# Two attention layers: heads split into high and low parts on 96 rows, against plain float32 heads on a quarter of the rows each

## What is computed

```python
scores = jnp.einsum('bqhd,bkhd->bhqk', q, k) * scale          # second layer, H = 16 heads of 8
scores = jnp.where(causal[None, None], scores, -inf)
attn = jax.nn.softmax(scores, axis=-1)
ctx = jnp.einsum('bhqk,bkhd->bqhd', attn, v)

ctx = X @ We.T                                                # third layer
influence = jnp.einsum('bqe,bke->bqk', ctx, ctx)
scores = jnp.einsum('bhqd,bhkd->bhqk', Q, K) * SCALE + 0.1 * influence[:, None]
attn = jax.nn.softmax(scores, axis=-1)
```

## Time and profile before

| | |
|---|---|
| median of 3 runs | 1821.09 us (1820.46 to 1821.55) |
| the profiled execution | 1818.61 us |
| its span, first to last instruction | 1816.9 us |
| busy: PE, DVE, ACT, POOL | 84%, 69%, 57%, 44% of the span |
| mean granted TensorE clock | 0.907 of full speed |

### The profile page before, as it was taken

How to read it: one execution, slowest core, us unless ns; L and a number is a source line. 1 busy time by engine, 2 the same in 40 slices (tenths; PEclk the granted TensorE clock), 3 DMA queues, 4 the chain that set the end, 5 groups by cost and what they waited for, 6 DMA issues and landing times. The chain is left out here.

```text
span 1816.9 us, 26731 instructions
## 1 busy us (share of the span) xinstructions
PE 1527.4 (84%) x8757; PEld 964.7 (53%) x8757; DVE 1249.6 (69%) x3212; ACT 1027.1 (57%) x1749; POOL 793.7 (44%) x902
## 2 busy tenths in 40 slices
PE   3788888689999999588769999999997686999980
PEld 1444555466666666343335545555553565777770
DVE  1656667467777777267777778777882574888875
ACT  2444555335666655424636677677675554777762
POOL 2244534435555544324741111222001576688875
PEclk8888989759999999788868999999998698999995
DMA  6800000212222221000244444443530022344415
GB/s 214 278 1 1 1 1 1 61 60 78 69 74 72 70 73 35 4 14 1 72 107 122 109 110 121 120 120 92 131 72 1 32 68 90 117 126 136 126 55 139
DMA packets 96201, 144.30 MB, mean 79 GB/s; under 512 B 31266, under 2 KB 59939, under 8 KB 91952
## 3 DMA queue, kind: packets, MB, share of 16 engines
q1 hardware_dynamic: 91072, 134.11, 26.5%
q0 software_dynamic: 4992, 8.48, 1.4%
HBM read 104.19 MB, written 57.48 MB: 89 GB/s over the span
## 5 line engine op out<-in xcount | busy, mean ns | idle before, releaser
L1176 DVE TENSOR_REDUCE ctx_nm<-ctx_s 128x1 f32<-128x512 f32 x496 | 320.0, 681 | 87.4 <-PE ctx_s L1310 86.6
L1176 DVE TENSOR_REDUCE rope_nm<-rope_s 128x1 f32<-128x128 f32 x496 | 223.5, 481 | 83.0 <-PE rope_s L1313 80.7
L1554 ACT ACTIVATE rope_probs<-rope_st 128x1024 f32<-128x1024 f32 (+1 forms) x256 | 172.2, 702 | 139.1 <-PE rope_st L1657 137.9
L1554 ACT ACTIVATE ctx_probs<-ctx_st 128x1024 f32<-128x1024 f32 x192 | 190.3, 1023 | 87.6 <-PE ctx_st L1657 84.1
L1310 PE MATMUL ctx_s<-att_kst,att_qst 96*128 96x512 f32 x496 | 210.9, 459 | 19.4 <-DVE ctx_nm L1176 8.4
L1310 PE MATMUL rope_s<-att_kst,att_qst 96*128 96x128 f32 x496 | 179.0, 392 | 8.8 <-PEq L120 5.5
L1657 PE MATMUL ctx_st<-att_qst,att_kst 98*128 98x512 f32 x512 | 164.7, 404 | 2.4 <-ACT ctx_probs L1554 1.5
L1419 POOL TENSOR_SCALAR_AFFINE_SELECT rope_probs<-rope_probs 128x256 f32<-128x256 f32 x256 | 98.1, 408 | 156.1 <-ACT rope_probs L1554 155.6
L1310 PEld LDWEIGHTS ctx_s<-att_kst,att_qst 96*128 96x128 f32 x496 | 95.8, 193 | 127.3 <-DVE ctx_nm L1176 51.0
L1657 PE MATMUL rope_st<-att_qst,att_kst 98*128 98x512 f32 (+3 forms) x512 | 141.2, 360 | 3.9 <-ACT rope_probs L1554 3.9
L2930 DVE TENSOR_TENSOR sw_hl<-sw_hf,sw_hh 128x512 fp32r<-128x512 f32 x124 | 128.5, 1037 | 0.1
(11 more groups left out here) (429 smaller groups left out, 3467.1 us busy)
## 6 DMA issues: line engine op xcount, KB each, us to landing
sw_raw<-in_L_ffn_all SPq DMA_DIRECT2D x24, 768.0 KB, 4.4
sw_xs<-in_pad SPq DMA_DIRECT2D x65, 260.0 KB, 9.5
rope_halves<-att_qk SPq DMA_DIRECT2D x24, 512.0 KB
ctx_halves<-att_qk SPq DMA_DIRECT2D x24, 512.0 KB, 5.7
att_qst<-ctx_contexts SPq DMA_DIRECT2D x32, 384.0 KB
att_kst<-ctx_contexts SPq DMA_DIRECT2D x32, 384.0 KB
att_qst<-rope_halves SPq DMA_DIRECT2D x32, 192.0 KB
att_kst<-rope_halves SPq DMA_DIRECT2D x32, 192.0 KB
```

The source lines that it names most:

```text
L1176: nc.vector.tensor_reduce(nm[:, g, j * T + t:j * T + t + 1], bank("s", b, n)[:, 0:keys], AXX, ALU.max, negate=True).then_inc(s_used, 1)
L1554: nc.scalar.activation(prob(n // GH % 2, n % GH)[:, u * units[0]:u * units[0] + units[u]], st_bank[u][:, 0:units[u]], ACT.Exp, scale=SCALE ...
```

## The change

The stacks become float32 tiles of 128 rows, `kst` and `qst` of shape [128, 2, NG, S], two batches deep. Head j of every group lies in quarter j of the rows: 8 rows of the head, in the third layer 16 of the context, and the guard in the last row of the quarter (row 31 of 32). `halves_of`, `halves_of_context`, `clear_stacks`, `guard_of_ones`, `cut_guard` and the float32r tiles go; `store_parts` and `load_stacks` write and read one batch whole, and `turn_guard` turns the maxima in one instruction. `prepare` sets the stacks and `vaug` at the start of the Performer's block on POOL.

A step now has four products, two heads by key and two by query, on four different quarters: those by key first, with keys c = i // 2 and heads of half i % 2, then those for the maximum, of the other half, with the query block whose width is the same; in the causal layer the two bfloat16 products (`hide_future` of PE) follow behind both. All other small products of the causal layer move from the bank `side` into the ring of three `s` banks; `st` becomes two tiles of two banks. The exponential takes two heads of one key block at a time. The Performer's `yT`, `yb`, `qT`, `kT`, `qp`, `qpT` and `hT` get tiles of their own.

```diff
-        self.kst, self.qst = sb("kst", [STACK + 2, NG, GH, S], F32R), sb("qst", [STACK + 2, NG, GH, S], F32R)
+        self.kst, self.qst = sb("kst", [P, 2, NG, S]), sb("qst", [P, 2, NG, S])
...
+        def scored(n):
+            i, k = n // 2, n % 2
+            return 2 * (1 - i % 2) + k, T - 1 - i // 2 if causal else i // 2
...
-                        (side if SIDE else ring).append((name, own, 0))
+                        ring.append((name, own, 0))
...
+            def load_stacks(b):
+                if causal and b == 0:
+                    sp.wait_ge(init, 4)
+                sp.wait_ge(stored, (b + 1) * NS)
+                for side, st in enumerate((qst, kst)):
+                    src = parts[b, side].rearrange("(d g j) t -> j d g t", g=NG, j=GH)
+                    for j in range(GH):
+                        row = QUARTER * j
+                        sp.dma_start(st[row:row + DH, b % 2], src[j]).then_inc(stacks_loaded[b % 2], 16)
+                        if not causal:
+                            sp.dma_start(st[row + DH:row + DH + CE, b % 2], contexts[b, side].unsqueeze(1).broadcast_to([CE, NG, S])).then_inc(stacks_loaded[b % 2], 16)
...
+            def prepare():
+                for k in range(2):
+                    nc.gpsimd.memset(qst[:, k], 0.0).then_inc(init, 1)
+                    nc.gpsimd.memset(kst[:, k], 1.0).then_inc(init, 1)
...
+            def turn_guard(b, g):
+                n = b * NG + g
+                dve.wait_ge(s_used, b * 64 + (g + 1) * GH * T)
+                if n:
+                    dve.wait_ge(m_stored, n * 16)
+                nc.vector.transpose(cutT[:], nm[:, g]).then_inc(mT_ready, 1)
...
+            def scores(b, pair):
...
+                two = (2 * pair, 2 * pair + 1)
+                g = pair // PAIRS
+                for n in two:
+                    vacated("s", b, n)
+                    j, t = scored(n % (GH * T))
+                    keys = P * (t + 1) if causal else S
+                    rows = slice(QUARTER * j, QUARTER * j + GUARD)
+                    last = nc.tensor.matmul(bank("s", b, n)[:, 0:keys], qst[rows, b % 2, g, t * P:(t + 1) * P], kst[rows, b % 2, g, 0:keys],
+                                            start=True, stop=not causal)
+                    if not causal:
+                        last.then_inc(s_ready, 1)
+
+            def hide_future(b, pair):
+                for n in (2 * pair, 2 * pair + 1):
+                    keys = P * (scored(n % (GH * T))[1] + 1)
+                    nc.tensor.matmul(bank("s", b, n)[:, keys - P:keys], identb[:], maskb[:], start=False, stop=True).then_inc(s_ready, 1)
...
+            def scores_by_key(b, g, i):
+                m = (b * NG + g) * PAIRS + i
+                if i == 0:
+                    pe.wait_ge(m_loaded[g % 2], (b * NG // 2 + g // 2 + 1) * 16)
+                if m >= 2:
+                    pe.wait_ge(p_ready, m - 1)
+                c, half = i // 2, i % 2
+                for k in range(2):
+                    rows = slice(QUARTER * (2 * half + k), QUARTER * (2 * half + k + 1))
+                    last = nc.tensor.matmul(st_bank[half][:, k, 0:width[c]], kst[rows, b % 2, g, c * P:(c + 1) * P],
+                                            qst[rows, b % 2, g, S - width[c]:S], start=True, stop=True)
                 last.then_inc(st_ready, 1)
...
-                    if within(ahead[0]) and not lead(ahead):
-                        score(*ahead, j, 2 * u)
                     now = keys_step(b, h)
                     if now:
-                        scores_by_key(now[0], now[1] // 8, j, u)
+                        scores_by_key(*now)
                     if within(ahead[0]) and not lead(ahead):
-                        score(*ahead, j, 2 * u + 1)
-                    if within(behind[0]) and u == 1 and j in (1, 3):
-                        weigh_values(*behind, j - 1)
-                        weigh_values(*behind, j)
+                        scores(ahead[0], ahead[1] * PAIRS + i)
+                    if within(ahead[0]) and not lead(ahead) and causal:
+                        hide_future(ahead[0], ahead[1] * PAIRS + i)
+                    if within(behind[0]) and i in (3, 7):
+                        weigh_values(*behind, i // 4 * 2)
+                        weigh_values(*behind, i // 4 * 2 + 1)
```

380 lines of the change are left out of this document (132 added, 248 removed).

## The result

| | before | after |
|---|---|---|
| median | 1820.78 us (4 runs, 1815.92 to 1821.55) | 2039.27 us (4 runs, 2035.32 to 2043.18) |
| ratio, 95% interval | | 1.1206, 1.1175 to 1.1238 |
| profiled execution: span | 1816.9 us | 2039.6 us |
| from first to last score of the causal layer | 373.2 to 728.0: 354.8 us | 378.5 to 857.0: 478.5 us |
| the same, third layer | 933.8 to 1366.5: 432.7 us | 1064.2 to 1585.5: 521.3 us |

The kernel is 12% slower. The prediction had 2012 us, slower, with a range of 1890 to 2160. Direction and range held, and so did the mechanism in the causal layer; in the third layer two of its steps did not, and the size fell 27 us short. Of the 222.7 us between the two spans, 123.7 lie in the causal layer (forecast 118), 88.6 in the third (69) and 10.4 in the seams and the rest (4).

The account below looks back on a forecast made before the run. PE was taken to set the causal layer's pace, DVE and PE the third's. Waits add 118 us causal, 69 third, 4 seams: 191 on the profiled 1818.6, the median 2.5 above, 2012 us, range 1890 to 2160.

Parts of the forecast that it names:

- the seams: Outside the two main blocks: +6 at the Performer's end, about 0 at the mixture's end, -2 for stack clearing; +4 us.
- The bound and the arithmetic: PE paces the causal layer, DVE and PE the third; four products cost 0.85 us of columns before and after.
- The causal chain: Causal layer: second product, bfloat16 product, first reduction, next second product wait in turn; 12.4 us a group.
- its smaller terms: Causal layer, per group: value products 2.4, hidden waits -1.5, transposes and projections in the ring +1.1, DVE's other work 0.65.
- the +6 for the start: Causal layer's first 28.8 us, at clock 0.52: two groups come to 37 us where 30 were counted.
- Rival 3: Clock stays at 1.2 GHz through both layers: +330 and +345, 2500 us; chance 0.09 in long stretches.
- The third layer: Longer stops at value products and small products, less the cuts, slower first steps: +69 us together.
- value products: Third layer: DVE stands 2.2 us at each of 62 places, 1.4 before; +50 us.
- transposes, projections: Third layer: eight a batch need four quarters drained and refilled, half a microsecond each; +31 us.
- the cuts: Third layer: the cuts go, 9.1 + 5.5 us of an engine that is the bound; -15 us.
- between value products DVE can run without a stop at 0.65 us a reduction: Third layer: the first bank can be read before the second is full, so no loss there.
- The signs: PE waits for `rope_nm` in over 200 places, DVE idles near 165 us in the third layer, starts within 0.05 us.

Follow-up runs that it names:

- a_short: The changed kernel with every reduction of both layers reading only the first 128 columns of its bank: 1903.06 us, ratio 1.0460 to the kernel before.
- a_nomask: The changed kernel without the bfloat16 products that hide later keys from the maximum: 1939.31 us, ratio 1.0652 to the kernel before.
- a_values4: The changed kernel with value products of one key block behind each second step, not two behind each fourth: 2006.13 us, ratio 1.1022.
- b_ring: The kernel before with the causal layer's small products in the ring of three banks instead of a bank of their own: 1846.36 us, ratio 1.0043.
- b_nomask: The kernel before without the bfloat16 products of the causal layer: 1822.48 us, ratio 0.9914.
- a_sf_halves: The changed kernel with scores for the maximum ahead of those by key, and the heads of the two halves exchanged: 2295.76 us, ratio 1.2488.
- a_scoresfirst: The changed kernel with products for the maximum and bfloat16 products ahead of the products by key: 2294.71 us, ratio 1.2592.

## Why the prediction was right, and where it was short

**The bound and the arithmetic** held. Four products on four row quarters start within 0.02 us and take 0.86 us of columns at 512, as the value products do on column quarters; a step of them alone takes 1.07 us, 0.11 of load and 0.11 of emptying around the columns:

```profile
1300.28 0.70 PE L1600 MATMUL ctx_st<-att_qst,att_kst 32*128 32x512 f32 x2
1300.29 0.70 PE L1280 MATMUL ctx_s<-att_kst,att_qst 31*128 31x512 f32 x2
...
1300.81 0.59 PE L1600 MATMUL ctx_st<-att_qst,att_kst 32*128 32x512 f32 x2
...
1301.35 0.66 PE L1238 MATMUL ctx_s<-ident,ctx_y 128*128 128x128 f32 x4
```

The page TensorE: Matmul & The Clock Gate of the Trainium skill, "Part 3: Packing small matmuls", gives 3.07 times; the trace has four times for the columns and 3.2 with load and emptying (4 x 0.86 over 1.07). The prediction counted both apart, so its value was right.

**The causal chain**, 12.4 us of a group, is shown: turns within 0.02 us behind a pair of the same width, its reduction taken away by a_short, its bfloat16 product by a_nomask, the cover that value products have by a_values4. A batch's four groups take 13.8, 14.2, 16.8 and 15.4 us wherever the clock is full, 15.05 on the mean, as forecast. That its smaller terms, which no run measured one by one in the changed kernel, are each right is not shown (the +6 for the start is 37 less 30, so 7; it measured 35.4 for the 37); b_ring had 0.3 us a group for one of them where 1.1 was counted, in a kernel with single products instead of pairs.

**The clock** took the causal layer past its forecast. Rival 3 had it low in long stretches or nowhere. In fact it fell seven times in the main part, for 3 to 7 us each, and came back. (The prediction also read from the earlier trace rows that before the change it "rose as the value products began"; in the trace it rose at 400.7 us, 1.2 us ahead of them, and after the change at 418.1, 4.7 us ahead.) The changed kernel, in stretches of 2.5 us, and what PE did as it fell:

```profile
642.50:645.00 2.50, 2.50 (x29) 1.38 (x26) 1.03 (x3) 1.54 (x4) 0.69 (x2) 1.00 0.00 0
645.00:647.50 2.50, 2.47 (x28) 1.49 (x26) 1.52 (x7) 1.76 (x6) 1.36 (x3) 0.85 0.00 0
647.50:650.00 2.50, 2.50 (x24) 0.74 (x16) 0.15 (x1) 0.00 (x0) 2.47 (x6) 0.50 0.07 13
650.00:652.50 2.50, 2.50 (x16) 0.82 (x12) 1.93 (x6) 1.83 (x2) 0.41 (x1) 0.96 0.02 3
```

```profile
644.46 0.28 PE L1288 MATMUL rope_s<-rope_maskb,rope_identb 128*128 128x128 bf16 x2
644.68 0.38 PE L1600 MATMUL rope_st<-att_qst,att_kst 32*128 32x128 f32 x2
...
645.62 0.28 PE L1288 MATMUL rope_s<-rope_maskb,rope_identb 128*128 128x128 bf16 x2
645.84 0.38 PE L1600 MATMUL rope_st<-att_qst,att_kst 32*128 32x128 f32 x2
```

Each of the seven falls comes within 0.6 us of the last bfloat16 product of the two steps of 128 columns that end a group; but all 29 groups end so, and 22 of them kept the clock. The value products that follow a fall run at 1.2 GHz. In all 27 of the 434.2 us passed at half clock. Beside groups at the same place in other batches, the groups with a fall are longer by 12 us together. Without the falls the layer would be at 467 us where 355 and 118 are 473, so the other terms together were 6 us too high.

**The third layer** is the part that failed: +88.6 for +69. DVE's idle time before its reductions, sorted by the PE products that started between the start of the last reduction and this one's:

| PE between | before | after | more | forecast |
|---|---|---|---|---|
| value products | 70.8 us | 115.2 us | 44 | 50 |
| transposes, projections | 10.2 us | 30.7 us | 20 | 31 |
| steps alone | 0.4 us | 18.2 us | 18 | 0 |
| the cuts, DVE's own time | | | 0 | -15 |

(The idle times are of the main part of the layer; +7 us more lie ahead of it, for +3. The line between the second row and the third is a matter of counting: from the end of the last reduction on, steps alone have 10.7 us before and 42.0 after.) Two steps of the forecast failed.

The first is "between value products DVE can run without a stop at 0.65 us a reduction". Here is a stretch without other work, and four reductions in a row of the kernel before:

```profile
1484.85 2.59 DVE L1153 TENSOR_REDUCE ctx_nm<-ctx_s 128x1 f32<-128x512 f32 x4 [2.05 <-PE ctx_s L1280]
1485.59 0.29 PEld L1280 LDWEIGHTS ctx_s<-att_kst,att_qst 31*128 31x128 f32 x2 [0.79 <-DVE ctx_nm L1153]
...
1487.65 1.29 DVE L1153 TENSOR_REDUCE ctx_nm<-ctx_s 128x1 f32<-128x512 f32 x2 [0.21 <-PE ctx_s L1280]
```

```profile
1333.26 2.48 DVE L1176 TENSOR_REDUCE ctx_nm<-ctx_s 128x1 f32<-128x512 f32 x4
```

The first reduction frees its bank at 1485.54, and the reduction of that bank's next use starts at 1486.75, 1.21 us later. The forecast's own terms give 0.06 + 0.11 + 0.86 + 0.22 = 1.25 for this, and DVE has two reductions to do meanwhile. Back to back their starts are 0.60 us apart, not 0.65, so these two take 1.21 us as well. Nothing is left over, and the next bank, freed at 1486.14, has its next reduction only 1.52 us later: DVE stops for 0.02 and then for 0.21 us. The main part has 55 stops like the first and 28 like the second. Why the second refill takes longer no run shows. a_short, whose reductions take 0.28 us, brought 64 us in this layer; it does not part these stops from those at the value products.

The second is the -15 for the cuts. They went, and all of DVE's instructions in this layer last 382.9 us after and 395.7 before. But back to back they overlap by 0.08 us, in 611 places before and in 461 after, so that the time in which DVE runs at all is the same, 346.4 and 346.0 us. The 60 cuts overlapped their neighbours and so cost about 10 us, not 15 (14.6 less 60 times 0.08). And DVE starts from rest 91 times more often than before, each time without the 0.08: about 7 us. Those took what the cuts gave.

**The seams** had 10.4 us for 4: 5.3 up to the causal layer's first score in the main block (forecast 4), 1.4 at the mixture's end (0), 3.7 behind the third layer, which the prediction did not count.

**The signs** it named: DVE idle before each pair, PE's wait for `rope_nm` (136 places in the list of waits, not over 200), DVE's idle time near 165 (175.9), starts within 0.05 us. All but the one count came.

## What to carry to other kernels

Equal columns are not equal time. Before putting products side by side, walk the ring: from a bank's release to the moment it is full again, and count what the reader has left to read meanwhile; here both were 1.21 us in the third layer, and DVE stopped even in quiet stretches. Products side by side lengthen that way, since all columns come late together (1.21 us from a product's start to its reduction, where one float32r product took 0.54), and here each product over all rows had 0.1 us of emptying on either side. And look at what PE's granted clock does in the thinnest stretch of the loop, not at its mean.

## What was not expected of the hardware

The granted clock changed with the order and the rows of the same instructions: 0.97 in the causal main part with keys first, 0.66 with scores first, 0.70 with scores first and other quarters (nearer 0.78 by the estimate above), 0.59 with a mask behind each score, 0.52 with all products on one quarter, while the page had PE busy for 100% of each of these stretches. The causal layer took 478, 757, 688, 872 and 1341 us with these. It was full without the bfloat16 products (a_nomask, 1.00), with short reductions (a_short, 1.00) and with the value products in four places (a_values4, 1.00), and 0.94 with thin ones. In the kernel before it was the other way round: 1.00 with the bfloat16 products, 0.97 without them (b_nomask). The experiment that should have shown shared quarters to be the cause (a_sf_halves) said no, and what separates 0.97 from 0.66 at the same work stays open. What is shown is that moving the same instructions within a step was enough to lose the clock for much of the layer. In the changed kernel it falls at the thin end of a group and is back after 3 to 7 us. With scores first (a_scoresfirst) its 17 falls come in steps of 128 columns too, but each lasts 20 to 51 us, through the wide steps that follow.
